# A graph layer on one core: 8 of 25 edge blocks gathered instead of 7, and the gathered groups placed in steps 3 to 14 of each phase

## The reference

```python
h = jnp.maximum(_layernorm(x, axis=-1), 0.0)
h = h @ W_node.T                       # 12500 x 16
rf = edge_attr_64 @ W_review.T         # 400000 x 64 -> 16
m = (h[src] + rf) * edge_weight1
return x + jax.ops.segment_sum(m, dst, num_segments=12500)
```

## Time and profile before

| | |
|---|---|
| median of 3 runs | 1734.9 us (1732.55 to 1735.05) |
| the profiled execution | 1738.82 us, of which the span from first to last instruction is 1737.1 us |
| granted TensorE clock, mean of the span | 0.913 |
| PE and DVE busy | 1402.1 and 1407.9 us, 81% each |
| ACT and POOL busy | 927.1 and 904.8 us |

### The profile page before, as it was taken

One profiled execution on the slowest core, in us unless ns is written; L12 is line 12 of the kernel. 1 busy time (PEld: TensorE's weight loads), 2 busy tenths in 40 slices (PEclk: granted clock), 3 DMA queues, 4 the chain that ended last, 5 costly groups with the idle time before them and its releaser, 6 DMA issues.

```text
span 1737.1 us, 93012 instructions
## 1 busy us (share of the span) xinstructions
PE 1402.1 (81%) x33622; PEld 1351.2 (78%) x33622; DVE 1407.9 (81%) x3305; ACT 927.1 (53%) x3944; POOL 904.8 (52%) x946
## 2 busy tenths in 40 slices
PE   0106998979797979798979797979797979898955
PEld 0106997979797979797979797979797979797953
DVE  7998887878787878787878787878787878787865
ACT  1102265656565656565656565656565656565653
POOL 3260375555565656565656565646565646564400
PEclk9657998999998989898989999999998989898966
DMA  3504354555454545454545454546454545454553
GB/s 110 94 4 103 86 128 118 134 125 127 119 130 114 136 109 136 110 134 120 129 115 133 115 139 109 139 105 144 105 139 117 136 110 135 117 133 110 135 98 54
DMA packets 507249, 202.22 MB, mean 116 GB/s; under 512 B 470303, under 2 KB 487428, under 8 KB 506492
## 3 DMA queue, kind: packets, MB, share of 16 engines
q1 hardware_dynamic: 475877, 186.76, 42.9%
q0 software_dynamic: 28000, 7.22, 4.5%
q10 hardware_dynamic: 2865, 1.61, 0.5%
HBM read 192.50 MB, written 2.99 MB: 113 GB/s over the span
## 4 chain that ended last, share of the span: by engine, by line
PE 50%; DVE 23%; issue 13%; DVEq 9%; ACT 3%; DMA 1%; ACTq 0%; SPq 0%
PE found L1162 35%; PE seg L1196 8%; DVEq L928 5%; DVE big L818 4%; PE seg L1186 3%; DVE found L880 2%; DVE found L874 2%; PE edge_h L1176 2%; DVE perm L913 2%; PE found L1170 1%; DVE by_rank L762 1%; DMA big<-in_src_dram 1%; DVE found L885 1%; ACT mid L636 1%; DVE big L763 1%
## 5 line engine op out<-in xcount | busy, mean ns | idle before, releaser
L574 POOL DMA_INDIRECT vals_p<-h_ext,idx_t x875 | 885.5, 1012 | 664.5 <-PE seg L1186 428.2
L1162 PE MATMUL found<-table,big 128*128 128x128 f16 (+6 forms) x18432 | 935.3, 214 | 77.3 <-DVE by_rank L940 37.5
L1162 PEld LDWEIGHTS found<-table,big 128*128 128x128 f16 x18432 | 893.3, 101 | 98.8 <-DVE by_rank L940 42.1
L636 ACT ACTIVATE mid<-mid,wgt_t 128x48 f32<-128x48 f16 x2250 | 534.4, 320 | 191.2 <-DVE mid L893 189.6
L818 DVE TENSOR_SCALAR big<-low_all,own 128x2004 f16<-128x2004 f16 x580 | 411.4, 751 | 3.7 <-DMA low_all<-low_dram 3.7
L636 ACT ACTIVATE sel_p<-hit_p,wgt_t 128x48 f32<-128x48 f16 x875 | 216.9, 322 | 290.1 <-DVE hit_p L893 262.4
L1196 PE MATMUL seg<-mid 128*47 128x48 f32 (+1 forms) x9000 | 270.1, 213 | 60.5 <-ACT mid L660 43.9
L1196 PEld LDWEIGHTS seg<-mid 128*47 128x47 f32 (+1 forms) x9000 | 241.4, 128 | 72.6 <-ACT mid L636 37.9
L932 DVE SCALAR_TENSOR_TENSOR acc<-seg,count_s,acc 113x48 f32 x450 | 120.7, 268 | 205.5 <-PE seg L1196 88.5
L913 DVE TENSOR_TENSOR perm<-edge_no,pos_t 128x1280 f16<-128x1280 f16 (+1 forms) x270 | 190.7, 706 | 0.0
L874 DVE COPY_PREDICATED found<-bits,found 125x512 f32<-125x512 uint8 (+1 forms) x270 | 152.5, 565 | 5.5 <-PE found L1162 5.4
(11 more groups left out here) (136 smaller groups left out, 550.4 us busy)
## 6 DMA issues: line engine op xcount, KB each, us to landing
low_all<-low_dram SPq DMA_DIRECT2D x144, 501.0 KB
mid<-in_edge_attr_dram SPq DMA_DIRECT2D x450, 160.0 KB
vals_p<-in_edge_attr_dram SPq DMA_DIRECT2D x180, 160.0 KB
vals_p<-h_ext,idx_t POOLq DMA_INDIRECT x875
big<-in_dst_dram SPq DMA_DIRECT2D x1, 1562.5 KB
big<-in_edge_weight_dram SPq DMA_DIRECT2D x1, 1562.5 KB
h_ext<-mid SPq DMA_DIRECT2D x2, 781.2 KB
big<-in_src_dram SPq DMA_DIRECT2D x1, 1125.0 KB
```

The source lines that it names most:

```text
L574: pool.indirect_dma_start(vals_p[:, slot_of(q), j, R:F], None, h_ext, bass.IndirectOffsetOnAxis(ap=idx_t[:, q * J + j:q * J + j + 1], axis=0),
L636: last = nc.scalar.activation(sel[:, j, :], hit[:, j, :], ACT.Copy, scale=wgt_t[:, bass.ds(tile + j, 1)])
L1162: last = nc.tensor.matmul(found[x % 2][:, r * P:r * P + n], hot[:, x // 2 % 2, a, col:col + P], rows, start=(a == 0 and part == 0), stop=( ...
```

## The change

The number of gathered blocks goes from 7 to 8 and that of sorted ones from 18 to 17, so that the loop has 16 passes and 200 groups are gathered. Each pass takes 12 gathered groups, in steps 3 to 14, one in each, and the first phase takes 8, in steps 8 to 15. The ring `RP` has six buffers.

```diff
-GATHERED = 7
-SORTED = 18
+GATHERED = 8
+SORTED = 17
 GROUPS = LISTS // J
...
-RP = 5
+RP = 6
...
-P_STEPS = [2, 4, 5, 7, 8, 10, 11, 13, 14, 15]
-FIRST_STEPS = [11, 12, 13, 14, 15]
+P_STEPS = [3, 4, 5, 6, 7, 8, 9, 10, 11, 12, 13, 14]
+FIRST_STEPS = [8, 9, 10, 11, 12, 13, 14, 15]
```

## The result

The changed kernel takes 1652.03 us (median of 3 runs, 1651.51 to 1653.97) against 1734.9 before: ratio 0.9521, interval 0.9495 to 0.9548. It is faster, and the time lies in the range, but 11 us over the 1641 of the forecast. The profiled execution took 1653.97 us, with a span of 1652.2; against the span of before that is -84.9 us, where the sum said -93.75. The other 2 us of the 11 come from the step from a profiled execution to the median: it stood 3.9 us above the median before and 1.9 after.

A forecast was written before the change was run, and what follows sets the result against it. DVE was taken to set the pass, PE having some 2.0 us to spare. One pass less -85.65, start -5.5, first phase +1.7, passes -4.3 sum to -93.75 us, giving 1641 us; range 1632 to 1668.

The forecast's parts named there:

- DVE sets the pass: Forecast case: work added on DVE lengthens a phase at once, PE has some 2.0 us to spare; 1632 to 1652 us, chance 0.60.
- POOL's wait at a phase's start: POOL idles 13.86 us there; two more gathered groups take 12.8 of it, so gathers stay hidden.
- the term of 1.8 us of delay against 2.0 of margin: PE in a pass: 1.8 us later against DVE by step 13, just within the copy's 2.0 us, so costing 0.
- its rival, at 0.28: PE, with ACT before it, sets the passes, each costing 1.2 to 2.4 us more: 1652 to 1684 us, chance 0.28.
- two sides of the SBUF: GpSimd DMAs and DVE's two-port operations block each other; bound of 0.44 us a pass, 7 in all, nothing in the sum.
- the change of a pass: DVE in each of 16 passes: hits 0.44, step 3's add -0.61, step 15's add -0.1, together -0.27 us.
- The add that leaves step 3: DVE in a pass: the waiting add between the two copies goes, gaining 0.61 us.
- the add that leaves step 15: DVE at a pass's end, behind PE's transposes: its going gains 0.1 us, between 0 and 0.27.
- the hits: DVE in a pass: 0.22 us for each gathered group, 0.44 us for the two added.
- The source load: Load of the sources for the sort, 20.92 us, loses one of 18 blocks: gain of 0.6 us, between 0 and 1.2.
- the first phase cost: First phase sums 8 gathered groups instead of 5, each 0.57 us on the chain: +1.7 us.
- the start's 2.4 us: Start, where DVE sorts one block less and the source load shrinks: forecast -5.5 us, bounds -3.7 and -6.6.

The follow-up runs named there:

- shift of 32: Changed kernel with 32 semaphore increments that nobody waits for put once at the head of DVE's program: 1649.07 us, ratio 0.9507 to the kernel before.
- other steps: Changed kernel with its twelve gathered groups in steps 2, 4 to 11, 13, 14 and 15 of a pass: 1649.61 us, ratio 0.9494 to the kernel before.
- PE at work in step 15: Changed kernel with the 40 matmuls of step 15's two sorted groups done twice on PE: 1648.59 us, ratio 0.9508 to the kernel before.

## Why the prediction was off, step by step

**What held.** DVE sets the pass, and in the middle of one PE's lookups are not waited for. Doubling three sums on PE cost nothing that can be measured, doubling DVE's hits cost 1.8 us a pass. One pass less gave its 85.65 us, the sort's operations came out as worked out (1292 ns for 1295), and no gather was waited for. POOL's wait at a phase's start went from 13.86 to 7.38 us; 12.8 of it should have gone, but a wait at one place is not all of POOL's idle time. That PE has room to spare was right by more than reckoned: the term of 1.8 us of delay against 2.0 of margin came out as 0.3 to 0.7, so its rival, at 0.28, had less for it than it was given.

**The rule on two sides of the SBUF.** The gathers' mean is 1031 ns after and 1012 before, with a median of 945 in both; in the passes alone it is 1015 and 1002, with DVE as busy as ever and a fifth more of them in a pass. Gathers of over 1.5 us stand mostly in the time of the sort (5 of 5 before, 10 of 15 after). The Trainium skill (SBUF — State Buffer, "SBUF: two separate sides") has DMAs from GpSimd and DVE's two-port operations block each other; if that is the cause of the long gathers, the change made it dearer by less than 2%. No run took it apart, and none says what it costs in both kernels alike.

**What failed: the change of a pass.** The term was -0.27 us and came out as +0.38. Three pieces of it were wrong:
- *The add that leaves step 3 was sized from one phase.* I took 0.61 us from copies that stood 1.17 us apart there. Over the passes of before they stand either 0.56 us apart (6 of 16) or 1.13 to 1.18 (10 of 16), with a mean of 0.94; the gain is 0.94 - 0.57 = 0.37, 0.24 us less than I took. With the shift of 32 it is there in full; in the changed kernel the gap at 58 takes it back.
- *The end of the pass.* I put a gain of 0.1 us on the add that leaves step 15. DVE's last `keep_valid` to the next mark became 0.26 us longer instead. A gathered sum that leaves PE's last step leaves PE idle for longer, the granted clock is at its lower level for more of the transposes behind it, and DVE waits for those that come late: 0.14 of the 0.26 us. Another 0.07 is there even where the transposes are fast, and 0.05 lies between the last split and the mark; these two I can't explain. I had taken work that leaves PE as costing nothing or gaining.
- *DVE's gaps.* The sum had no term for them. Shifting them gives back 0.1 to 0.2 us.

The two kinds of pass in the first of these go by the clock as well. Two passes of before, the 6 us ahead of the first copy (columns: stretch, us, PE, PEld, DVE, ACT and POOL busy, PEclk, DMA share, GB/s). The first is the one of the earlier trace rows, with 1.17 us between the copies; the second has the copies shown, 0.56 us apart:

```profile
389.40:395.40 6.00, 6.00 (x138) 5.91 (x137) 5.18 (x15) 4.74 (x24) 0.16 (x1) 0.72 0.24 76
304.60:310.60 6.00, 6.00 (x173) 5.92 (x171) 5.17 (x15) 4.72 (x24) 1.33 (x2) 1.00 0.50 142
310.60 0.42 DVE L880 COPY_PREDICATED found<-bits,found 125x256 f32<-125x256 uint8 x1
311.16 0.30 DVE L885 COPY_PREDICATED found<-bits,found 125x128 f32<-125x128 uint8 x1
```

In all 10 slow passes the clock was at its lower level for about 3 of these 6 us, in none of the 6 fast ones at all. PE then ends the sums of step 2 some 1.4 us later, DVE waits for them ahead of the add, and the register load for the add comes behind the first copy instead of ahead of it. So the add did wait, as the prediction says, but only where the clock had been low: the phase that I read closely was of the slow kind.

Together 0.24 + 0.36 + 0.15 = 0.75 us, against 0.65 missed; the hits, 0.14 us cheaper than taken, make up the difference. With effects of 0.1 us a pass (1.6 us in all, half of what a measurement can tell), I would not read this closer.

**What was off by its size alone.** The source load, outside its bounds (2.5 us for at most 1.2), gained 1.9 us more than taken; the first phase cost 2.9 us for 1.7. That the time came within 11 us of the forecast is in part luck: without the start's 2.4 us it would be over 13.

**What stays open.** Where DVE's gaps come from; why the clock has fallen in one pass and not in the next after the same idle time; and the 0.12 us at the end of the pass. The best versions (other steps, PE at work in step 15, a shift of 32, ratios 0.9494 to 0.9508) lie 0.1 to 0.3% under the changed kernel (0.9520), at the edge of what can be told.

## What to carry to other kernels

A term that is multiplied by the number of passes must be read over all passes, by mean and spread, and not from the one phase that was read closely: 0.24 us from one instance became 4 us. If its values fall into two groups, as here, ask what differs between the passes; the granted clock of the stretch ahead is the first thing to look at. When a chain alternates between two engines, don't ask which has the larger share of it; measure the slack at the point where one hands over to the other, and load each engine once to see which pays. And work taken off an engine that waits is not free: look at what that engine runs right behind the wait, and at which clock.

## What the runs showed of the hardware that was new to me

DVE loses some 0.35 us about every 128 instructions, register and semaphore instructions counted, at places that move with instructions put in once at the head of its program; where DVE waits anyway, it costs nothing.

f32 transposes of 125 columns take 277 ns at a granted clock of 1.00 and 415 ns at 0.50. The mean over the span hides this: it lies between 0.904 and 0.918 in all of these kernels, while the share of transposes at the lower level goes from 0% to 88% with PE's idle time ahead of them (0.5 to 3.7 us).

The same add costs DVE nothing or 0.6 us by where the register load ahead of it (0.30 us in the trace) falls: under the operation of line 818, or behind a wait and so in the open.
